# K-projection blocks of the even heads moved to every second softmax step, and the output projection on two PSUM banks, in a transformer layer on eight cores

## What is computed

```python
Q = (X @ Wq.T + bq).reshape(B, S, H, d_head) * scale
K = (X @ Wk.T + bk).reshape(B, S, H, d_head) * scale
V = (X @ Wv.T + bv).reshape(B, S, H, d_head)
scores = jnp.einsum('bqhd,bkhd->bhqk', Q, K)
scores = jnp.where(causal[None, None], scores, -jnp.inf)
attn = jax.nn.softmax(scores.astype(jnp.float32), axis=-1).astype(X.dtype)
out = jnp.einsum('bhqk,bkhd->bqhd', attn, V).reshape(B, S, D)
return out @ Wo.T + bo
...
x = x + attn(layernorm(x))
x = x + ffn(layernorm(x))      # silu(gate) * up, then down
```

## Time and profile before

| what | value |
|---|---|
| median, lowest, highest of 3 runs | 2429.64, 2429.05, 2683.72 us |
| the profiled execution's own time | 2431.9 us |
| span of its slowest core (core 7) | 2430.4 us |
| TensorE matmul busy | 2053.6 us, 84% |
| VectorE (DVE) busy | 787.6 us, 32% |
| ScalarE (ACT) busy | 704.8 us, 29% |
| chain that ended last | PE 76%, DVE 8%, ACT 7%, issue 5%, DMA 3% |

### The profile page before, as it was taken

The page is one execution under the profiler, slowest core; times in us unless marked ns, Lnnn a source line. Parts: engine busy times, 40 slices in busy tenths (PEclk is TensorE's granted clock), DMA queues, the critical chain, the costliest instruction groups (busy, mean ns, idle before and its releaser), DMA issues.

```text
span 2430.4 us, 31335 instructions; the slowest of 8 cores (2404.2 to 2430.4 us)
## 1 busy us (share of the span) xinstructions
PE 2053.6 (84%) x12000; PEld 1119.5 (46%) x12000; DVE 787.6 (32%) x1540; ACT 704.8 (29%) x1556; POOL 95.4 (4%) x175
## 2 busy tenths in 40 slices
PE   1895678878787878888877878998999999899999
PEld 1443445555464646464643333443444444344444
DVE  4435033332324242424243233332332233223322
ACT  2333154454535363635352011210121012101110
POOL 1000000000000000000000001100001000101100
PEclk9996788888888988888877888999999999999999
DMA  7555201010101010110111005661455045606612
GB/s 204 156 130 148 35 8 20 18 27 18 27 18 27 18 27 18 19 26 18 27 27 53 35 35 87 118 123 28 86 105 103 11 84 108 113 1 113 113 44 122
DMA packets 29667, 151.75 MB, mean 62 GB/s; under 512 B 3392, under 2 KB 3472, under 8 KB 16976
## 3 DMA queue, kind: packets, MB, share of 16 engines
q0 software_dynamic: 23760, 107.79, 24.7%
q1 hardware_dynamic: 5760, 41.95, 5.0%
HBM read 248.82 MB, written 8.39 MB: 106 GB/s over the span
## 4 chain that ended last, share of the span: by engine, by line
PE 76%; DVE 8%; ACT 7%; issue 5%; DMA 3%; DVEq 0%; POOL 0%; ACTq 0%; POOLq 0%
PE PS L847 13%; PE PS L788 13%; PE PS L818 12%; PE PS L407 10%; PE PS L435 7%; PE PS L352 5%; PE PS L650 5%; ACT PSA L509 5%; PE PS L566 4%; DVE SM L488 4%; PE PS L474 3%; DVE BNS L277 2%; PE PS L533 2%; PE PS L480 1%; DMA A<-wup 1%
## 5 line engine op out<-in xcount | busy, mean ns | idle before, releaser
L488 DVE TENSOR_REDUCE SM<-PS 128x1 f32<-128x512 f32 x320 | 204.3, 686 | 454.0 <-PE PS L474 428.9
L847 PE MATMUL PS<-A 128*128 128x512 bf16 x1024 | 245.4, 383 | 20.4 <-DVE A L834 20.4
L435 PE MATMUL PS<-A 128*128 128x512 bf16 x1024 | 235.1, 383 | 19.7 <-DMA A<-wkp 16.9
L407 PE MATMUL PS<-A 128*128 128x256 bf16 x2048 | 237.6, 281 | 1.5 <-ACT A L322 1.5
L407 PEld LDWEIGHTS PS<-A 128*128 128x128 bf16 x2048 | 205.9, 101 | 31.6 <-issue 1.8
L818 PE MATMUL PS<-A 128*128 128x512 bf16 x960 | 210.1, 379 | 0.0
L799 ACT ACTIVATE A<-PS,SGP 128x512 f32<-128x512 f32 x88 | 60.5, 687 | 491.6 <-PE PS L788 471.1
L788 PE MATMUL PS<-A 128*128 128x512 bf16 x896 | 199.9, 384 | 3.1 <-DVE A L740 3.1
L509 ACT ACTIVATE PSA<-PS,SM 128x512 bf16<-128x512 f32 x224 | 151.1, 685 | 103.4 <-DVE SM L497 102.0
L566 PE MATMUL PS<-A,PTS 128*128 128x128 bf16 x640 | 72.8, 261 | 123.2 <-DVE SM L516 62.6
L847 PEld LDWEIGHTS PS<-A 128*128 128x128 bf16 x1024 | 100.7, 99 | 144.5 <-issue 26.4
(11 more groups left out here) (107 smaller groups left out, 2189.7 us busy)
## 6 DMA issues: line engine op xcount, KB each, us to landing
A<-xown SPq DMA_DIRECT2D x16, 1024.0 KB, 5.4
A<-x SPq DMA_DIRECT2D x16, 1024.0 KB, 6.1
A<-wgp POOLq DMA_DIRECT2D x16, 1024.0 KB, 9.3
A<-wup POOLq DMA_DIRECT2D x16, 1024.0 KB, 7.9
A<-wdp POOLq DMA_DIRECT2D x32, 512.0 KB, 11.6
A<-wqp POOLq DMA_DIRECT2D x8, 1024.0 KB, 9.5
A<-wvp POOLq DMA_DIRECT2D x8, 1024.0 KB, 9.0
A<-wkp POOLq DMA_DIRECT2D x8, 1024.0 KB, 8.8
```

Of the source, the lines that this page charges most:

```text
L407: last = t.matmul(bankw(b, 256), h1F[:, c * 2048 + kt * 128:c * 2048 + (kt + 1) * 128], wvbuf[:, c * 256:(c + 1) * 256], start=(c == 0), s ...
L435: last = t.matmul(bank(6), wkbuf[:, c * 256 + hp2 * 128:c * 256 + (hp2 + 1) * 128], h1F[:, c * 2048 + kt * 512:c * 2048 + (kt + 1) * 512], ...
L488: OP("dve", lambda v, rr=rr, base=base, r2=r2: v.reduce_max(sm(24 + 4 * r2 + rr), bank(base + rr), axis=AX.X), reads=[bank(base + rr)], wr ...
L847: last = t.matmul(bank(b), aF[:, k * 1024 + tt * 128:k * 1024 + (tt + 1) * 128], wd_tile(k)[:, dm * 512:(dm + 1) * 512], start=(k == 0), s ...
```

## The change

The two edits:

```diff
@@ -605,8 +605,8 @@
                     softmax_exp(idx, j)
                     if prev2 is not None:
                         evac_at(*prev2)
-                    if hp == 0 and idx >= 4:
-                        kproj_kt(1, idx - 4)
+                    if hp == 0 and idx % 2 == 1:
+                        kproj_kt(1, idx // 2)
                     if hp == 1 and pr < 7 and idx >= 4:
                         kproj_kt(0, idx - 4, prv=pr + 1)
                     if prev is not None:
@@ -642,7 +642,7 @@
         for tt in range(NO):
             xload(xo_in.ap()[tt * 128:(tt + 1) * 128, :], tt % 2, queue="sp")
             for dm in range(4):
-                bko = dm
+                bko = dm % 2
 
                 def omm1(t, b=bko, tt=tt, dm=dm):
                     last = None
```

## The result

The changed kernel has a median of 2508.27 us over 9 runs, the kernel before one of 2431.58 over 10 runs, the first three included; the ratio is 1.033, with a 95% interval of 1.030 to 1.036. It is slower by 3.3%, clear of noise. The forecast was 2495.

A forecast was written before the change was run, and what follows sets the result against it. Slowest core 7 sets the time; in attention heads TensorE is not full and its clock moves. 8.1 us in eight heads, 65, plus 0.8 for banks gives 2498 profiled, 2495 as median; range 2438 to 2520.

The forecast's parts named there:

- likeliest case: Even attention heads: K blocks in odd steps restart at low clock, +8.1 us a head, 2495 us in all; chance 0.60.
- new bank wait, once: Output projection, row tile 1: with two banks the third group waits for the first's addition, +0.8 us once.
- the four restarts: K blocks in odd steps of even heads start at low clock: 1.2 us extra once, 1.9 three times.
- step 1: Even head, second of eight query-tile steps (counted from 0): K block outlasts the 1.56 us wait it covers, +2.3 us.
- steps 3, 5 and 7: Later odd query-tile steps of an even head: full-clock TensorE work plus a 1.9 us restart, +1.9 us each.
- the fourth rival: Transposes do not count for the clock, blocks start wholly cold: 11.2 us a head, 2519 us; chance 0.06.
- step 2: Even head, query-tile step without a K block: same chain, scores and AV at full clock, -0.3 us.
- The second rival: Even heads: only the first two K blocks pay, then the clock holds; 3.9 us a head, 2461 us; chance 0.19.
- The third: Rival: evenly spread work keeps the clock up in even heads, no restart paid; 0.5 us a head, 2434; chance 0.13.
- The chain part: Even heads, steps 4 and 6: softmax chain sets them, their K blocks cost nothing; losing them gives 0.0 and +0.4 us.
- step 7's block: Last K block of an even head stays there, so the K weight load waiting for it keeps its place.
- waits for line 593: Sign of a right forecast: waits for this ScalarE evacuation, ahead of AV in attention, grow; no total size given.

The follow-up runs named there:

- the filler run: The changed kernel plus 16 matmuls, whose result nobody reads, in each of steps 2, 4 and 6 of the even heads; profiled execution 2464.4 us.

## Why the prediction was right, and where it was off

The forecast was its likeliest case, by its own mechanism: K blocks restarted at the low clock in odd steps, nothing gained in even ones, banks near nothing. By its steps, in the head from 855.21 against that of the earlier trace rows:

| step | forecast | measured |
|---|---|---|
| 1 | +2.3 | +3.3 (12.1 against 8.8) |
| 2 | -0.3 | -0.3 |
| 3 | +1.9 | +2.2 |
| 4 | 0.0 | -0.2 |
| 5 | +1.9 | +2.3 |
| 6 | +0.4 | +0.4 |
| 7 | +1.9 | +2.2 |
| head | +8.1 | +9.9 |
| new bank wait, once | +0.8 | +0.7 |

The mis-sized terms are the four restarts. In step 1 I had written 1.2, on the reasoning that slow transposes ahead of the block leave less of the restart for it; the block measured 5.95 us, 2.3 more than at full clock, and with a filler ahead the whole of it vanished. Transposes count, as the fillers of transposes show, but those in step 1 did not bring the clock back ahead of the block; why is not shown, and behind the same ones the block takes 4.3 to 4.5 us in four later heads of the filler run. In steps 3, 5 and 7 I took 1.9, from the lower part of 1.7 to 2.5 in the earlier trace rows, and 2.2 to 2.3 were measured. All eight even heads together have 76.5 us more against 65 forecast; these 11.5 us and the odd heads' 2.0 are the gap of 13 between 2495 and 2508.

By its number alone the forecast was not the best: the fourth rival's price of 11.2 us a head gave 2519, which is 11 from the measured time, where the forecast is 13 away. That the forecast had the better mechanism is known from the experiments and not from the time. Its own range of 2470 to 2515 does not follow from restarts of 1.3 to 2.5 either: put into the sum for all four blocks, these give about 2482 and 2520.

One reading of the profile was wrong without harm. The DVE reduction named for the 4.75 us wait in step 2 had not long ended: it runs from 959.13 for 0.16 us and so ends at 959.29, at the same time as the evacuation at line 593.

The second rival (the clock holds from step 4 on) is out: the clock is 0.70 and 0.71 in steps 5 and 7. The third (evenly spread blocks keep it up) is out for the same reason; blocks do keep the clock up when they stand in the steps with the waits, as the runs with blocks in the even steps show. Of the fourth the reason fell.

The chain part held: steps 4 and 6 hardly changed length when they lost their blocks, so these were free before. That step 7's block keeps the K weights' load in place held too: the one wait of a K block for that load is 15.9 us, 16.9 before. The odd heads are 48.4 us on average, 48.1 before. The waits for line 593 grew from 56.3 to 95.2 us in all, as the prediction had named as a sign.

## What to carry to other kernels

Where a chain of small steps through several engines leaves TensorE idle, put independent dense work into the step with the longest wait and not where it spreads evenly by number: in this kernel it was free there, and kept the clock up for what follows. When judging such a move, price the work behind each newly opened wait at the low clock, not only the wait. A filler of matmuls whose result nobody reads, put into the waits, is a quick test of whether a stretch is slow for its clock or for its order.

## What was not expected of the hardware

Adding 384 matmuls took 62 us off the even heads of core 7. The clock's cost is not fixed: K blocks behind a wait took 0.2 to 2.3 us more than at full clock, and one filler in step 4 changed the V projection from 29.6 to 27.9 us. And transposes kept the clock at full level just as matmuls did, K blocks at 3.62 us behind them, and in the last head of one run it came back in the midst of them.
